# Keeping the second half's residual in device memory: added from reloaded rows instead of by TensorE

## What is computed

```python
x = layernorm(x + attention(x))      # linear attention, 16 heads, 64 random features
x = layernorm(x + ffn(x))
# ffn: silu(x Wg + bg) * (x Wu + bu) @ Wd + bd
#      + sum over 4 heads of the best 8 of 1024 experts:
#        silu(x . down[i]) * softmax(score)[i] * up[i]
```

## Time and profile before

| | |
|---|---|
| median of 3 runs | 3632.07 us (3629.95 to 3634.01) |
| the profiled execution | 3635.19 us, its span 3633.4 us |
| mean granted TensorE clock | 0.991 |
| PE busy | 3549.2 us, 98% |
| DVE busy | 2585.7 us, 71% |
| ACT busy | 1981.3 us, 55% |
| POOL busy | 1514.3 us, 42% |
| HBM read, written | 41.04 MB, 16.78 MB |

### The profile page before, as it was taken

One profiled execution on the slowest core, in us unless ns is written; L12 is line 12 of the kernel. 1 busy time (PEld: TensorE's weight loads), 2 busy tenths in 40 slices (PEclk: granted clock), 3 DMA queues, 4 the chain that ended last, 5 costly groups with the idle time before them and its releaser, 6 DMA issues.

```text
span 3633.4 us, 52250 instructions
## 1 busy us (share of the span) xinstructions
PE 3549.2 (98%) x19420; PEld 2929.1 (81%) x19420; DVE 2585.7 (71%) x5554; ACT 1981.3 (55%) x2886; POOL 1514.3 (42%) x1012
## 2 busy tenths in 40 slices
PE   8789999999999999999999999999999999999988
PEld 6668888888888888888888888888888888888877
DVE  4577777777777777777777777777677777777773
ACT  4455465555555555556555555555655554555551
POOL 0354344443344434444433444443444434555440
PEclk9899999999999999999999999999999999999999
DMA  3000000000000000000000000000000000000000
GB/s 118 18 12 18 13 13 12 18 18 12 12 18 12 18 18 13 12 18 13 18 18 13 13 13 18 18 14 17 13 12 18 18 7 12 13 13 12 7 6 12
DMA packets 23339, 61.17 MB, mean 17 GB/s; under 512 B 5552, under 2 KB 10032, under 8 KB 23088
## 3 DMA queue, kind: packets, MB, share of 16 engines
q1 hardware_dynamic: 18480, 41.04, 3.6%
q0 software_dynamic: 4608, 16.78, 1.1%
HBM read 41.04 MB, written 16.78 MB: 16 GB/s over the span
## 4 chain that ended last, share of the span: by engine, by line
PE 90%; DVE 3%; ACT 3%; POOL 1%; issue 1%; SPq 0%; DMA 0%; DVEq 0%; ACTq 0%; POOLq 0%
PE ring L639 28%; PE y_bank L732 12%; PE y_bank L734 11%; PE step_bank L554 6%; PE step_bank L562 6%; PE step_bank L666 6%; PE step_bank L639 5%; PE step_bank L598 3%; PE step_bank L656 3%; PE step_bank L548 3%; PE step_bank L590 3%; PE step_bank L712 3%; PE y_bank L728 1%; POOL grid L461 1%; DVE prob L1120 1%
## 5 line engine op out<-in xcount | busy, mean ns | idle before, releaser
L461 POOL TENSOR_TENSOR grid<-ex 128x1024 f32<-128x1024 f32 x512 | 1066.3, 2090 | 999.2 <-DVE prob L1117 364.3
L732 PE MATMUL y_bank<-wd_sb,gate 128*128 128x256 f32 x2048 | 621.6, 385 | 0.0
L734 PE MATMUL y_bank<-up_sb,wexp 128*128 128x256 f32 x2048 | 609.1, 379 | 0.0
L1107 DVE SCALAR_TENSOR_TENSOR grid<-grid,best 128x1024 f32<-128x1024 f32 x256 | 329.0, 1285 | 328.2 <-POOL grid L461 327.3
L1120 DVE SCALAR_TENSOR_TENSOR prob<-grid,narrow,prob 128x1024 f32<-128x1024 f32 x256 | 450.7, 1760 | 7.9
L639 PE MATMUL ring<-x1T_hl,downT_hl 128*128 128x512 f32 x1536 | 421.3, 409 | 17.2 <-ACT gate L883 17.2
L639 PE MATMUL ring<-x1T_hl,wg_hl 128*128 128x512 f32 x1536 | 428.8, 414 | 3.1 <-DVE gate L1136 3.1
L734 PEld LDWEIGHTS y_bank<-up_sb,wexp 128*128 128x128 f32 x2048 | 389.1, 190 | 52.8
L639 PE MATMUL ring<-x1T_hl,wu_hl 128*128 128x512 f32 x1536 | 422.2, 410 | 0.0
L732 PEld LDWEIGHTS y_bank<-wd_sb,gate 128*128 128x128 f32 x2048 | 354.0, 190 | 50.8 <-issue 22.7
L883 ACT ACTIVATE gate<-ring,bg_sb 128x512 f32<-128x512 f32 x256 | 176.3, 689 | 396.7 <-PE ring L639 395.0
(11 more groups left out here) (159 smaller groups left out, 5920.9 us busy)
## 6 DMA issues: line engine op xcount, KB each, us to landing
xb<-in_L_attn_x SPq DMA_DIRECT2D x34, 512.0 KB, 3.7
out_y<-x POOLq DMA_DIRECT2D x32, 512.0 KB, 3.0
xa<-in_L_attn_x SPq DMA_DIRECT2D x30, 512.0 KB, 3.7
prob<-in_L_ffn_down_embed SPq DMA_DIRECT2D x1, 1024.0 KB, 5.8
prob<-in_L_ffn_Wg SPq DMA_DIRECT2D x1, 1024.0 KB, 8.6
prob<-in_L_ffn_Wu SPq DMA_DIRECT2D x1, 1024.0 KB, 10.5
wd_sb<-in_L_ffn_Wd SPq DMA_DIRECT2D x1, 1024.0 KB, 11.4
up_sb<-in_L_ffn_up_embed SPq DMA_DIRECT2D x1, 1024.0 KB, 12.1
```

The source lines that it names most:

```text
L461: pool.tensor_tensor(grid[:, h % 2], bcast(ex[:, h, 0:NX].unsqueeze(2), [P, NX, NK]), bcast(ex[:, RH + h, 0:NK].unsqueeze(1), [P, NX, NK]) ...
L732: pe.matmul(rows, gate[:, c % 2, t * P:(t + 1) * P], wd_sb[:, c, :], start=(c == 0 and t % 2 == 0), stop=False, skip_group_check=True)
L734: mm = pe.matmul(rows, wexp[:, c % 2, t * P:(t + 1) * P], up_sb[:, c, :], start=False, stop=(c == C - 1), skip_group_check=True)
L1107: marks["keep", h] = rt_steps.mark(dve.scalar_tensor_tensor(out=g, in0=g, scalar=best[:, h, TOP - 1:TOP], in1=g, op0=ALU.is_ge, op1=ALU.mult))
```

## The change

The normalised rows x1 of each group are stored to a new tensor x1_kept in device memory, by SP, when norm1 is done. Two iterations later SP loads them back into the tile x1, when the transposes of the newer group have been made and the former output rows have been stored. POOL adds the bias bd to them, as the first thing of its block 0 and behind the bias addition of xb. VectorE's y block moves from the start of block 0 to behind ff_wexp(0), and adds the y banks to these rows instead of the bias to the banks. POOL's norm_scale of the y block moves behind the middle places of block 0, and the store of the output rows moves to the front of block 1. TensorE's identity matmuls are gone. VectorE has a wait for x1_stored before it writes x1 again.

```diff
--- before.py
+++ after.py
@@ -68,6 +68,8 @@
     x_groups = x.rearrange("b s d -> (b s) d").rearrange("(g p t) d -> g p t d", p=P, t=T)
     out_groups = out.rearrange("b s d -> (b s) d").rearrange("(g p t) d -> g p t d", p=P, t=T)
 
+    x1_kept = nc.dram_tensor("x1_kept", [NG, P, T, D], F32).ap()
+
     with ExitStack() as ctx:
         def sb(name, *shape, dt=F32):
             return ctx.enter_context(nc.sbuf_tensor(name, list(shape), dt))
@@ -164,6 +166,7 @@
 
         ring_full, ring_act = sem("ring_full"), sem("ring_act")
         h_ready = sem("h_ready")
+        x1_stored, res_loaded, res_ready = sem("x1_stored"), sem("res_loaded"), sem("res_ready")
         y_full, y_read, y_dve = sem("y_full"), sem("y_read"), sem("y_dve")
         ln2_pool, rstd2_ready, y_ready, y_stored = (sem("ln2_pool"), sem("rstd2_ready"),
                                                     sem("y_ready"), sem("y_stored"))
@@ -380,7 +383,7 @@
                     sp.dma_start(lane.x[:], x_groups[2 * r + k]).then_inc(lane.loaded, 16)
 
             def body(it, par, kv, at, rt, ff, last, batch):
-                a, m = it, it - ATTN_LAG
+                a, m, f = it, it - ATTN_LAG, it - LAST_LAG
                 if kv:
                     sp.wait_ge(*full("kv", a - 1 if a > 2 * FILL else a - 2, "turn", 1))
                     sp.dma_start(xa[:], x_groups[a]).then_inc(xa_loaded, 16)
@@ -390,6 +393,14 @@
                     else:
                         sp.wait_ge(*drained("at", m - 1, "wo", 1))
                     sp.dma_start(xb[:], x_groups[m]).then_inc(xb_loaded, 16)
+                if 0 < m <= NG:
+                    sp.wait_ge(x1_ready, m * T)
+                    sp.dma_start(x1_kept[m - 1], x1[:]).then_inc(x1_stored, 16)
+                if last:
+                    sp.wait_ge(*full("at", min(m, NG) - 1, "next", 1))
+                    sp.wait_ge(x1_stored, min(m, NG) * 16)
+                    wait(sp, y_stored, f * 16)
+                    sp.dma_start(x1[:], x1_kept[f]).then_inc(res_loaded, 16)
 
             schedule(sp, body, lambda b: None)
 
@@ -474,24 +485,28 @@
 
                 for c in range(C):
                     t, odd = divmod(c, 2)
+                    if last and c == 0:
+                        pool.wait_ge(res_loaded, (f + 1) * 16)
+                        pool.tensor_tensor(x1[:], x1[:], bcast(bd_sb[:].unsqueeze(1), [P, T, D]),
+                                           ALU.add).then_inc(res_ready, 1)
+                    if last and c == 1:
+                        pool.wait_ge(y_ready, (f + 1) * T)
+                        pool.dma_start(out_groups[f], y_sb[:]).then_inc(y_stored, 16)
                     kv_adds(KV_FIRST[c])
                     at_adds(AT_EARLY[c])
                     if rt and odd:
                         spread(t, 2)
-                    if last and c == 0:
-                        norm_scale(y_dve, (f + 1) * Y_STEPS, ln2_pool, f, mv2, rstd2, rstd2_ready)
                     kv_adds(KV_EARLY[c])
                     at_adds(AT_MID[c])
                     if rt and odd:
                         spread(t, 3)
                     if at and c == 6:
                         norm_scale(at_dve, (m + 1) * AT_STEPS, ln1_pool, m, mv1, rstd1, rstd1_ready)
+                    if last and c == 0:
+                        norm_scale(y_dve, (f + 1) * Y_STEPS, ln2_pool, f, mv2, rstd2, rstd2_ready)
                     if rt and not odd:
                         spread(t, 0)
                     kv_adds(KV_LATE[c])
-                    if last and c == 1:
-                        pool.wait_ge(y_ready, (f + 1) * T)
-                        pool.dma_start(out_groups[f], y_sb[:]).then_inc(y_stored, 16)
                     if rt and not odd:
                         spread(t, 1)
                     at_adds(AT_LATE[c])
@@ -721,14 +736,6 @@
                         pe.wait_ge(*drained("pt", n, c))
                     for t in (2 * pair, 2 * pair + 1):
                         rows = y_bank[pair][:, (t % 2) * D:(t % 2 + 1) * D]
-                        if c == C - 2:
-
-                            for k in range(KD):
-                                for part in range(2):
-                                    pe.matmul(rows[:, k * P:(k + 1) * P],
-                                              x1T_hl[:, par, part, k, t * P:(t + 1) * P], ident_r[:],
-                                              start=False, stop=False, skip_group_check=True)
-
                         pe.matmul(rows, gate[:, c % 2, t * P:(t + 1) * P], wd_sb[:, c, :],
                                   start=(c == 0 and t % 2 == 0), stop=False, skip_group_check=True)
                         mm = pe.matmul(rows, wexp[:, c % 2, t * P:(t + 1) * P], up_sb[:, c, :],
@@ -1040,6 +1047,8 @@
                         rows = x1[:].rearrange("p t (i h w) -> p t i h w", i=4, h=4)[:, :, j]
                         if j == 0 and last:
                             dve.wait_ge(y_stored, (f + 1) * 16)
+                        elif j == 0:
+                            wait(dve, x1_stored, m * 16)
                         dve.wait_ge(*full("at", m, kind, j))
                         if j:
                             dve.wait_ge(*drained("at", m, kind, j - 1))
@@ -1145,13 +1154,10 @@
                 def y_rows():
 
                     dve.wait_ge(y_full, (f + 1) * C)
-
-                    if m:
-                        dve.wait_ge(*full("at", min(m, NG) - 1, "next", 1))
-                    wait(dve, y_stored, f * 16)
+                    dve.wait_ge(res_ready, f + 1)
                     for i in range(2):
                         dve.tensor_tensor(y_sb[:, 2 * i:2 * i + 2, :], pair(y_bank[i]),
-                                          bcast(bd_sb[:].unsqueeze(1), [P, 2, D]), ALU.add).then_inc(y_read, 1)
+                                          y_sb[:, 2 * i:2 * i + 2, :], ALU.add).then_inc(y_read, 1)
                     dve.wait_ge(y_read, (f + 1) * 2)
                     statistics(y_sb, stats, mv2, y_steps)
 
@@ -1170,8 +1176,6 @@
 
                 for c in range(C):
                     t, odd = divmod(c, 2)
-                    if last and c == 0:
-                        y_rows()
                     uses(KV_FIRST[c])
                     if c == 1 and it <= NG and it % BG == 0:
                         blocks(it // BG - 1)
@@ -1190,6 +1194,8 @@
                         norm1_stats()
                     if ff:
                         ff_wexp(c)
+                    if last and c == 0:
+                        y_rows()
                     if rt and odd:
                         add_head(t, 1), add_head(t, 2)
                     uses(KV_LATE[c])
```

## The result

| | before | after |
|---|---|---|
| median | 3632.39 us | 3694.46 us |
| the profiled execution's span | 3633.4 us | 3695.5 us |
| mean granted TensorE clock | 0.991 | 0.983 |

The changed kernel takes 1.0172 times as long, with a 95% interval of 1.0155 to 1.019. It is 62 us slower; the forecast was 18 us slower, and the forecast's range ended at 3672.

A forecast was written before the change was run, and what follows sets the result against it. TensorE, busy for 98% of the span, was taken to bound the kernel. New waits of 68.4 and 5.4 us less 55.5 us of matmuls gave +18.3 us, so 3650.4 us from 3632.07; range 3608 to 3672.

The forecast's parts named there:

- The matmuls, 1.79 us per group: TensorE's sixteen 128-column matmuls per group (line 728) removed: 1.79 us saved in each of 31 groups, 55.5 us.
- Store and reload for nothing: Both 512 KB DMAs on SP's queue, 3.7 us each, cost nothing, with 9 us of cover before POOL needs the rows.
- The chain, 3.6 us in a plain iteration: Block 0: late rows, y block, stretched norm2, choose(0), ACT's mask and relu; PE stalls 3.6 us at qp 1, 19 iterations.
- Rival A: norm2 gets the port first or doesn't collide; qp 1 waits 2.0 instead of 3.6 us; 3615.5 us, chance 0.20.
- I add nothing: After PE's 3.6 us stall, the others' lag of about 1 us is below the cover in blocks 1 to 3: nothing added.
- rival C: The lag doesn't end in block 1; PE waits again, 1.4 us in 22 iterations; 3681 us, chance 0.09.
- Cost 0: Six fold iterations: POOL waits 7.13 us for exponentials before its first spread, so the chain is covered and norm2 meets nobody.

The follow-up runs named there:

- e1: Kernel before without its 512 identity matmuls, residual left out of the result; 0.9847 of before, 3579.4 us.
- e9: e6 with spread(0,0) also held until norm2 is done; 0.9884 of before, 3590.4 us.
- e2: Changed kernel with POOL's addition to the reloaded rows moved ahead of that of xb; 1.0007 of before, 3638.6 us.
- e3: Changed kernel in which POOL starts spread(0,0) only when norm2 is done; 1.0039 of before, 3649.6 us.
- e5: Changed kernel with POOL adding to the reloaded rows first and holding spread(0,0) until norm2 is done; 0.9905 of before, 3596.3 us.
- e8: Changed kernel with TensorE repeating the two matmuls of qp 0 three more times in the 19 plain iterations; 1.0172 of before.
- e7: Kernel before, residual still by TensorE, with y block, norm_scale and store at the change's places; 1.0026 of before.
- e10: Changed kernel with VectorE's blocks() moved from behind choose(0) to ahead of the y block; 1.0162 of before.
- e6: Changed kernel with reloaded rows added first on POOL, and y block, norm_scale and store at their old places; 0.9924 of before, 3601.6 us.
- e11: The changed kernel itself measured once more, nothing altered; 1.0168 of before.
- e4: Changed kernel with TensorE repeating the two matmuls of qp 0 five more times in the 19 plain iterations; 1.0167 of before.

## Why the prediction was right in its sign and wrong in its size

- **The matmuls, 1.79 us per group:** measured 1.78 in the plain iterations (e1). Right there, but it was taken for 31 groups, and in iterations 33 and 34 e1 gets back 0.43 us in the mean, as PE then waits 1.48 us for the gate where it waited 0.57.
- **Store and reload for nothing:** right; the rows are there 7 us before POOL comes, and in e9 they are early enough for the front of VectorE's list.
- **The chain, 3.6 us in a plain iteration:** measured 3.62, with norm2 at 2.93 (forecast 2.9). Right at each link; e2, e3 and e5 take it apart. Rival A did not come about, as norm1's timeline had said: POOL had the port first. The Trainium skill (SBUF — State Buffer, section "SBUF: two separate sides") has it that the one that starts first holds the shared pair for its whole instruction; the trace agrees, with norm2 at 2.93 us beside a spread and 1.38 us in e3.
- **"I add nothing" behind block 1:** this is the step that failed. It had three parts.
  - In plain iterations PE, 3.6 us late at qp 1, is 3.9 us late behind its products of line 681 in block 2 (after against e1, iteration 9), and then there is TensorE's clock. The shortest of them are 111.07 long, 2.16 more than before and not 1.81; the mean is 111.60. The 0.5 between goes with the clock drops: the iterations without one don't have it, and in e8, with the idle stretch halved, 17 of 19 don't. No term of the sum had the clock.
  - In iterations 33 to 35 rival C came true, in block 3. PE is 2.4 us late in block 1 (forecast 1.8), and then it waits 2.45 us for the gate, since ACT's exponentials of scores(1), behind which the gate stands, begin only when VectorE's late list has come to them:

```profile
3269.82 2.70 PE L654 MATMUL ring<-x1T_hl,downT_hl 128*128 128x512 f32 x6 [2.45 <-ACT gate L890]
...
3265.78 1.28 ACT L866 ACT_TABLE_LOAD   x1 [6.80 <-DVE ex L1094]
```

  In iteration 33 PE is 2.7 us late ahead of this wait, 4.6 behind it and 6.1 behind the clock drop that follows; less the matmuls it is 4.7 us of an iteration for which I had counted none. The saving was out of reach here too: before, this wait was 0.57 us long, so there was no cover at all, and leaving out the matmuls by itself makes it 1.48 (e1). Its price was in the text, +1.4 us, but I gave it a chance of 0.09 for all iterations and not of one for those with the shortest block list.
  - Behind iteration 34 the same happens: 4.4 us instead of -1.8.
- **"Cost 0" in the folds:** wrong, in the premise that POOL would find the exponentials late. That holds only where TensorE's clock falls behind the fold. An iteration of after with a fold (24):

```profile
2253.09 1.22 PE L671 MATMUL step_bank<-qT_hl,rw_hl 128*128 128x512 f32 x2 [2.12 <-DVE kv_blocks L1020]
...
2247.20 1.90 POOL L472 TENSOR_TENSOR grid<-ex 128x1024 f32<-128x1024 f32 x1
```

  The spread starts at 2247.20, in the moment of norm2, as in a plain iteration. Before, the products behind the fold ran at the lower clock in six of the seven folds. In the same iteration, the window of before is (columns as in the earlier trace rows)

```profile
2210.00:2215.00 5.00, 5.00 (x16) 3.10 (x14) 0.87 (x2) 1.56 (x4) 0.45 (x1) 0.66 0.33 105
```

  with PE busy throughout and the clock at 0.66, and ACT's exponentials ended 10.7 us behind POOL's xb addition; here these products ran at full clock and it was 9.0. So the cover that I read from the earlier trace rows was partly the low clock. The same trace of after has the counter-case: in iteration 20 the clock falls right behind the fold, the exponentials end at 10.7, norm2 meets nobody and PE doesn't wait:

```profile
1801.56 1.38 DVE L1167 TENSOR_SCALAR x<-x,mv,rstd 128x256 f32<-128x256 f32 x4
...
1802.76 2.27 POOL L472 TENSOR_TENSOR grid<-ex 128x1024 f32<-128x1024 f32 x1 [1.31 <-ACT ex L866]
```

  It takes 111.8 us, 1.8 less than before's 113.6, just as forecast.

  Where the clock stays up, behind choose(0) stands blocks(), whose bank PE wants for qp 0: 2.1 us of waiting, which the forecast didn't see (1.5 in e7, by the place alone). With it gone (e10) such an iteration is 0.9 us shorter. The fold's iteration without a clock drop took 111.91 us before (iteration 8) and takes 112.52 after (8 and 12), 0.6 more and not 1.8 less. The others with a first half took 113.6 before (12, 16, 20, 24, 28, each with a drop). Now 12 has no drop; 16 has it somewhat later than before and takes 112.65, 20 has it as before; 24 and 28 have it behind the new wait and take 114.1 and 114.2. Why it is at one place or the other stays open.
- **The range** ended at 3672, though rival C stood at 3681. Rival and forecast had the same sign and the same cause, a lag longer than its cover, and so more of C belonged into the range.

## What to carry to other kernels

Work taken from the engine that sets the pace brings it sooner to everything it asks of the others, so the covers must be read anew, at every place behind a late link and in the iterations with the fewest instructions (e1's wait for the gate, 0.57 to 1.48 us with no list touched). A cover read in a stretch at the low clock may be gone at the full one. A block of a hand-written list that is moved has to be followed to the last link with its new neighbours on the shared port: here its four last instructions went from 1.38 to 2.93 us and, from after to e2, a small one ahead of it from 0.21 to 2.15 us, though nobody touched them. The edit that paid was to put the reloaded rows first, to keep the waiting block where it stood (e6, 0.992 of before, where the change as made is 1.017) and to hold the spread until norm2 is done (e9, 0.988).

## What the runs showed of the hardware that was not expected

- TensorE's clock fell to its lower level, 1.2 GHz (a mean of 0.66 over 5 us, so 1.7 us missing), behind idle stretches of 2.7 us, but only in 11 of 19 plain iterations that have the same wait (12 and 13 of 19 in e11 and e10); with the idle stretch cut to about 1.4 us by filler, in none of 19 (e8). Of ten waits of 1.3 us in block 2, over six runs, four were followed by a drop (two of three in e4, one each in e2 and e5, none in e6, e8 and e11).
- The drops behind the fold's small products, in six of the seven folds of the kernel before and 1.7 us each, come with PE busy for the whole of the 5 us around them (5.00 of 5.00 in the window above).
- A VectorE subtraction of 128 x 64 with both inputs in SBUF takes 0.21 us alone, and 2.15 us when POOL's 128 x 1024 addition has begun 0.3 us before it (e2), or 1.55 when 0.9 us before it (before): both times it ends within 0.1 us of that addition's end. The Trainium skill (SBUF — State Buffer, section "SBUF: two separate sides") has this for VectorE instructions with two SBUF inputs; the trace agrees.
- 114 to 190 matmuls more, put where TensorE waits anyway, cost nothing that could be measured.
